# Token mixer with centred small matrices: output held channel by token, channel sums and output projection in fp32, no transposes

## The reference, cut to what matters

```python
x = x + mixer(ln(x)); t = tokens(x); t = t + moe0(ln(t))
x = x + divisive_norm_conv(ln(x)); t = tokens(x); t = t + moe1(ln(t))

def mixer(u):                      # per image, 256 tokens
    xbcdt = u @ W_in               # 128 values, 16 B, 16 C, 8 dt
    dt = softplus(xbcdt[dt] + dt_bias);  dA = dt * (-exp(A_log))
    KV = einsum('bls,blhp->bhsp', B, V * dA)
    y  = einsum('bls,bhsp->blhp', C, KV) + V * D_param
    y  = (y - mean(y)) / sqrt(var(y) + 1e-5) * ln_gamma + ln_beta   # over 128 channels
    return y @ W_out               # 128 -> 64
```

## Time and profile before

| | us |
|---|---|
| median of 3 runs (lowest, highest) | 723.84 (723.64, 726.32) |
| the profiled execution, its own time | 722.71 |
| span of its profile | 720.9 |
| busy: PE, DVE, ACT, POOL | 522.0, 523.4, 378.9, 283.1 |
| mean granted PE clock, of full speed | 0.924 |

### The profile page before, as it was taken

How to read it: one execution, slowest core, us unless ns; L and a number is a source line. 1 busy time by engine, 2 the same in 40 slices (tenths; PEclk the granted TensorE clock), 3 DMA queues, 4 the chain that set the end, 5 groups by cost and what they waited for, 6 DMA issues and landing times.

```text
span 720.9 us, 10179 instructions
## 1 busy us (share of the span) xinstructions
PE 522.0 (72%) x3778; PEld 247.9 (34%) x3778; DVE 523.4 (73%) x926; ACT 378.9 (53%) x440; POOL 283.1 (39%) x240
## 2 busy tenths in 40 slices
PE   2314674578787988798777978797879876975766
PEld 1213232233333433344334333343334332431322
DVE  3266267859798879987988898889979796556413
ACT  2113712467476555756575657664766564643532
POOL 2122146125434463635452653365254433333013
PEclk9999965699998999999999999999999998998788
DMA  4600600063205140505032502450044005500130
GB/s 67 102 3 1 133 0 1 2 132 74 47 1 134 31 89 15 123 13 117 15 83 53 120 16 55 79 119 16 21 99 100 19 17 117 116 18 1 43 76 30
DMA packets 27841, 41.50 MB, mean 58 GB/s; under 512 B 11792, under 2 KB 19088, under 8 KB 27792
## 3 DMA queue, kind: packets, MB, share of 16 engines
q1 hardware_dynamic: 27152, 38.75, 26.2%
q0 software_dynamic: 640, 2.10, 1.0%
HBM read 38.22 MB, written 2.62 MB: 57 GB/s over the span
## 4 chain that ended last, share of the span: by engine, by line
DVE 37%; DMA 23%; PE 13%; issue 10%; POOL 8%; SPq 5%; ACT 4%; POOLq 0%; DVEq 0%; ACTq 0%
DMA WB<-w_scratch 19%; DVE nacc L1134 6%; PE yP L861 4%; PE hP L845 4%; SPq L402 3%; DMA w_scratch<-wTs 3%; DVE YW L1181 2%; POOL stat_c L486 2%; PE sA L760 2%; DVE xsplit L971 2%; PE sA L770 2%; DVE xcen_b L964 2%; POOL stat_b L486 2%; DVE xnrm L964 1%; POOL stat_d L486 1%
## 5 line engine op out<-in xcount | busy, mean ns | idle before, releaser
L691 ACT ACTIVATE H<-hP,b 128x1024 f32<-128x1024 f32 x192 | 209.3, 1111 | 82.4 <-PE hP L845 80.8
L861 PE MATMUL yP<-H,w 128*64 128x512 f32 x768 | 205.6, 618 | 28.5 <-DVE ACC L1181 25.1
L845 PE MATMUL hP<-xT,w 128*64 128x512 f16 x1536 | 212.4, 401 | 4.1 <-ACT H L691 4.0
L556 POOL TENSOR_TENSOR ACC<-ACC,YW 128x512 f32<-128x512 f32 x96 | 125.5, 1313 | 192.1 <-DVE YW L1181 192.1
L845 PEld LDWEIGHTS hP<-xT,w 128*64 128x64 f16 x1536 | 83.6, 114 | 128.0 <-issue 70.8
L1181 DVE SCALAR_TENSOR_TENSOR YW<-yP,b,WB 128x512 f32<-128x512 f32 x96 | 71.3, 744 | 31.9 <-PE yP L861 31.9
L861 PEld LDWEIGHTS yP<-H,w 128*64 128x64 f32 x768 | 54.0, 141 | 71.8 <-issue 38.1
L1134 DVE SCALAR_TENSOR_TENSOR nacc<-PAD,taps,nacc 128x256 f32<-128x256 f32 x112 | 60.5, 540 | 3.7
L1181 DVE SCALAR_TENSOR_TENSOR ACC<-yP,b,WB 128x512 f32<-128x512 f32 x32 | 23.1, 746 | 50.5 <-DMA WB<-w_scratch 50.5
L540 POOL TENSOR_SCALAR nrg<-nacc,go_col 128x512 f32<-128x512 f32 x8 | 12.6, 1573 | 69.1 <-ACT nacc L659 69.1
L578 ACT ACT_TABLE_LOAD x23 | 29.5, 1283 | 9.7 <-DVE nacc L1134 7.9
(11 more groups left out here) (144 smaller groups left out, 775.6 us busy)
## 6 DMA issues: line engine op xcount, KB each, us to landing
WB<-w_scratch SPq DMA_DIRECT2D x32, 1024.0 KB, 10.0
X<-in_x SPq DMA_DIRECT2D x8, 256.0 KB, 12.0
out<-X POOLq DMA_DIRECT2D x8, 256.0 KB, 2.8
H<-in_L_ffn_W SPq DMA_DIRECT2D x2, 512.0 KB, 6.6
H<-in_L_ffn_W SPq DMA_DIRECT2D x2, 256.0 KB, 4.2
w<-in_L_ffn_W SPq DMA_DIRECT2D x1, 512.0 KB, 4.9
w_scratch<-wTs SPq DMA_DIRECT2D x16, 32.0 KB, 1.8
w<-in_L_ffn_W SPq DMA_DIRECT2D x1, 256.0 KB, 4.1
```

What stands on the lines that cost most here:

```text
L556: pool.tensor_tensor(ACC[l][:, cols], ACC[l][:, cols], YW[:, u % 4, :], ALU.add).then_inc(summed, 1)
L691: nc.scalar.activation(H[:, s % RING, :], hP[s % 2][:, :], ACT.Gelu, bias=b1[l][:, e * ch + c:e * ch + c + 1], scale=1.0 / WS)\
L845: mm = nc.tensor.matmul(hP[s % 2][b * C:(b + 1) * C, hf * HALF:(hf + 1) * HALF], w1[l][:, sp, w, b * C:(b + 1) * C], xT[l][g % 2][:, hf * ...
L861: mm = nc.tensor.matmul(yP[hf][a * C:(a + 1) * C, :], w2[l][:, (2 * j + a) * ch + c, :], H[:, (2 * ch * j + 2 * c + a) % RING, hf * HALF:( ...
```

## The change

The output y of the mixer is now made channel by token. V * D becomes a product: the columns of W_in that give V, times D, centred over the 128 channels (`wd`, two fp16 parts), times `xTa`. `KV` is centred over its 128 columns too, so that y comes out of PSUM with mean zero: two fp16 products and one fp32 product of 256 columns for each image. ACT takes y's square and y itself out of PSUM. PE sums the squares over the channels with a column of ones, in fp32 (`y_sums`); DVE scales the sums, POOL takes the power -1/2. `mix_out` multiplies y with `wout_g` in fp32, 8 products instead of 32, and DVE scales the result by the power (first operation) and adds X0b (second). Yd, Yc, ysplit, the transposes `turn_hi` and `turn_lo` and layer norm n's steps on DVE, ACT and POOL are gone. KV's centring is on DVE (`state`: a reduction and one operation) instead of ACT's copy.

The slots: `AB_LEAD` goes from 42 to 36. Modulo 24, on DVE: centre_a 12, sums_a 19, norm_a 22, decay 9, values 10, state 11, y_sums 16, mix_out and what follows it where it was. On PE: proj0, 1, 2 in 5, 7, 8 (before 23, 1, 2), c_cols 9 (3), state 11 (5), y0 12 (6), y1 14 (8), y_sums 16, mix_out 17 (17). On ACT: squares of a 17 (13), proj0, 1, 2 in 5, 6, 7 (23, 0, 1), c_cols and decay 9 (3), y0 12, y1 14. On POOL: low part of a 21 (15), X0b 14 (8), the new power y_sums 16. The start-up is six slots shorter.

```diff
@@ tables
-    ab=dict(turn_a=12, proj0=17, proj1=19, proj2=20, c_cols=21, state=23, y0=24, y1=26, turn_hi=32,
-            turn_lo=34, mix_out=35, turn_b=38, gate=41, send=43),
+    ab=dict(turn_a=13, proj0=17, proj1=19, proj2=20, c_cols=21, state=23, y0=24, y1=26, y_sums=28,
+            mix_out=29, turn_b=32, gate=35, send=36),
...
-    ab=dict(centre_a=0, sums_a=6, norm_a=10, decay=21, values=22, y0=25, y1=27, centre_n=28, sums_n=29,
-            norm_n=30, mix_out=35, centre_b=35, sums_b=36, norm_b=37, top2=41, weights=41),
+    ab=dict(centre_a=0, sums_a=7, norm_a=10, decay=21, values=22, state=23, y_sums=28, mix_out=29,
+            centre_b=29, sums_b=30, norm_b=31, top2=35, weights=35),
...
-AB_LEAD = 42
+AB_LEAD = 36
@@ PE
+                    for t in range(2):
+                        for s in range(2):
+                            nc.tensor.matmul(sA[:, t * PIX:(t + 1) * PIX], wd[:, s, :],
+                                             xTa[:, hf * HALF + t * PIX:hf * HALF + (t + 1) * PIX],
+                                             start=(s == 0), stop=False)
+                        mm = nc.tensor.matmul(sA[:, t * PIX:(t + 1) * PIX], KVs[q, t * INNER:(t + 1) * INNER],
+                                              ctS[q, t * PIX:(t + 1) * PIX], start=False, stop=True)
...
+                elif k == "y_sums":
+                    pe.wait_ge(*a_read(k, g))
+                    pe.wait_ge(yev.sem, yev.at(g))
+                    for t in range(T):
+                        mm = nc.tensor.matmul(sA[:, t:t + 1], ysq[:, t * P:(t + 1) * P], ones[:, 0:1],
+                                              start=True, stop=True)
...
                     for t in range(T):
-                        for n in range(4):
-                            mm = nc.tensor.matmul(sA[:, t * C:(t + 1) * C], yT[:, n // 2, t * P:(t + 1) * P],
-                                                  wout[:, n % 2, :], start=(n == 0), stop=(n == 3))
+                        mm = nc.tensor.matmul(sA[:, t * C:(t + 1) * C], yT[:, t * P:(t + 1) * P], wout_g[:, :],
+                                              start=True, stop=True)
@@ ACT
+                elif k in ("y0", "y1"):
+                    hf = int(k[-1])
+                    cols = slice(hf * HALF, (hf + 1) * HALF)
+                    act.wait_ge(ymm.sem, ymm.at(g, hf + 1))
+                    nc.scalar.activation(ysq[:, cols], sA[:, :], ACT.Square, scale=1.0 / WS).then_inc(yev.sem, 1)
+                    nc.scalar.activation(yT[:, cols], sA[:, :], ACT.Copy, scale=1.0 / WS).then_inc(yev.sem, 1)
@@ POOL
+                elif k == "y_sums":
+                    pool.wait_ge(yvar.sem, yvar.at(g))
+                    pool.tensor_tensor(stat["n"][:, 3, :], stat["n"][:, 2, :], neg_half[:, :], ALU.pow)\
+                        .then_inc(yrs.sem, 1)
@@ DVE
+                elif k == "state":
...
+                    v.tensor_reduce(kv_mean[:, :], state, AX, ALU.add).then_inc(kvC.sem, 1)
+                    dve.wait_ge(kvC.sem, kvC.at(g, 1))
+                    v.scalar_tensor_tensor(out=KVs[:, :].rearrange("p (m n) -> p m n", m=2),
+                                           in0=kv_mean[:, :].unsqueeze(2).to_broadcast([64, 2, INNER]),
+                                           scalar=-1.0 / INNER, in1=state, op0=ALU.mult, op1=ALU.add)\
+                        .then_inc(kvC.sem, 1)
+                elif k == "y_sums":
+                    dve.wait_ge(ysm.sem, ysm.at(g))
+                    v.tensor_scalar(stat["n"][:, 2, :], sA[:, 0:T], 1.0 / INNER, 1e-5, ALU.mult, ALU.add)\
+                        .then_inc(yvar.sem, 1)
...
-                    v.scalar_tensor_tensor(out=X1[g % 2][:, :, :], in0=sA[:, :].rearrange("p (t c) -> p t c", t=T),
-                                           scalar=1.0 / WS, in1=X0b[:, :, :], op0=ALU.mult, op1=ALU.add)\
+                    dve.wait_ge(yrs.sem, yrs.at(g))
+                    v.tensor_tensor(X1[g % 2][:, :, :], sA[:, :].rearrange("p (t c) -> p t c", t=T),
+                                    per_tile(stat["n"][:, 3, :], C), ALU.mult).then_inc(x1s.sem, 1)
+                    dve.wait_ge(x1s.sem, x1s.at(g))
+                    v.tensor_tensor(X1[g % 2][:, :, :], X1[g % 2][:, :, :], X0b[:, :, :], ALU.add)\
                         .then_inc(x1v.sem, 1)
```

More of the change, by code:

```diff
@@ L61 @@
 ACT_AT = dict(
-    ab=dict(sums_a=7, turn_a=12, proj0=17, proj1=18, proj2=19, c_cols=21, decay=21, state=23, sums_n=28,
-            turn_hi=32, turn_lo=33, sums_b=36, turn_b=37, top2=41, send=42),
+    ab=dict(sums_a=5, turn_a=13, proj0=17, proj1=18, proj2=19, c_cols=21, decay=21, y0=24, y1=26,
+            sums_b=30, turn_b=31, top2=35, send=36),
     cd=dict(sums_c=1, turn_c=4, norms=9, sums_d=11, turn_d=14, top2=17, send=18),
@@ L72 @@
 POOL_AT = dict(
-    ab=dict(sums_a=7, norm_a=9, decay=25, state=26, sums_n=30, norm_n=31, sums_b=34),
+    ab=dict(sums_a=7, norm_a=9, state=26, y_sums=28, sums_b=29),
     cd=dict(sums_c=1, norm_c=2, scale=8, sums_d=12),
@@ L76 @@
 SP_AT = dict(
-    ab=dict(decay=22, send=41),
+    ab=dict(decay=22, send=35),
     cd=dict(send=21),
@@ L319, in sums_until @@
             return 6 * (u // 8) + max(0, u % 8 - 1)
-        A_USES = ("turn_a", "proj0", "proj1", "proj2", "c_cols", "state", "y0", "y1", "turn_hi", "turn_lo", "mix_out",
+        A_USES = ("turn_a", "proj0", "proj1", "proj2", "c_cols", "state", "y0", "y1", "y_sums", "mix_out",
                   "turn_b", "gate", "send")
@@ L341, in a_read @@
             count, k = {"turn_a": (trS["a"], 1), "proj0": (pjS, 1), "proj1": (pjS, 2), "proj2": (pjS, 3),
-                        "c_cols": (ctC, 1), "state": (kvS, 1), "y0": (yv, 1), "y1": (yv, 2), "turn_hi": (trS["n"], 1),
-                        "turn_lo": (trS["n"], 2), "mix_out": (x1v, 1), "turn_b": (trS["b"], 1), "gate": (gv[0], 1),
+                        "c_cols": (ctC, 1), "state": (kvC, 2), "y0": (yev, 2), "y1": (yev, 4), "y_sums": (yvar, 1),
+                        "mix_out": (x1s, 1), "turn_b": (trS["b"], 1), "gate": (gv[0], 1),
                         "send": (wts[0], 1)}[name]
@@ L614, in ab @@
                     act.wait_ge(ct.sem, ct.at(g))
-                    nc.scalar.activation(ctS[:, :], sA[0:64, :], ACT.Copy, scale=1.0 / WS).then_inc(ctC.sem, 1)
+                    nc.scalar.activation(ctS[:, :], sA[0:64, :], ACT.Copy).then_inc(ctC.sem, 1)
                 elif k == "decay":
@@ L766, in ab @@
                     pe.wait_ge(*a_read(k, g))
[L767 removed]
+                    pe.wait_ge(kvC.sem, kvC.at(g))
                     q = slice(32 * hf, 32 * hf + STATE)
[L769 to L778 removed]
+                    for t in range(2):
[5 more added lines that the diff above has]
+                                              ctS[q, t * PIX:(t + 1) * PIX], start=False, stop=True)
```

99 lines of the change are left out of this document (31 added, 68 removed).

## The result

The changed kernel takes 740.25 us (median of 4 runs, 737.01 to 742.88), the kernel before 723.74 in the runs beside it (722.27 to 726.32): ratio 1.022, 95% interval 1.016 to 1.028. Slower, as forecast (736, range 712 to 747). The profiled execution took 737.01, its span is 735.2: 14.3 more than before, where the working had 14.0. It is the fastest of the four; by medians the difference is 16.5, and the forecast lay 12.3 above 723.74.

The account below looks back on a forecast made before the run. DVE's nearly gapless work and two DRAM weight transfers bound each frame. Start-up -12.3, frame 0 +1.5, frames 1 to 5 +22.8, frame 6 +2.0 sum to +14.0, 736.7 profiled; forecast 736 us, range 712 to 747.

Parts of the forecast that it names:

- What bounds, and what leaves: Per 24-slot frame (four images), DVE work and two weight transfers set time; the removed normalisation, mostly under a transfer, gains nothing.
- C + D = 28.4, no change: First layer 0 scaling, through layer 1 gate weights (C), to first layer 1 scaling: C's 2.5 gain spent, 28.4 +/- 0.8 us.
- D: Layer 1 weights' DRAM transfer up to first layer 1 scaling, 15.3 us before; PE's new tail, not the DMA, ends it.
- A + 4.55: First layer 1 scaling to layer 0 gate weights (A), 30.7 us before, DVE almost without gap: grows 4.55 a frame.
- B unchanged: Layer 0 weights' DRAM transfer, from gate weights to first layer 0 scaling (B): keeps 15.9 us.
- Start-up -12.3: Up to the first layer 0 scaling: X1 ready 16 earlier, 3.7 given back to norm a steps, so 12.3 us shorter.
- X1 at 42.6: At start-up, X1 ready at 42.6 instead of 58.7 after DVE's operations behind the second X, 16 us earlier.
- Frame 0 +1.5, frame 6 +2.0, end 0: Frame 0, without layer 1, +1.5 us; frame 6, with no group behind it, +2.0; frame 7 and end, without mixer, 0.
- The signs: DVE busy about 6 us less a frame, late transposes releasing layer 1 scaling, weights' copy over 1 late, layer 0 scaling about 78.
- The faster one (702): PE's tail ahead of the first layer 1 scaling doesn't decide, y_sums and pow hide: 702 us, chance 0.22.
- the limit of 15.8: PE's work between layer 1 send and last transposes: below some 15.8 us the faster rival was to hold.
- Rival 3 (clock): PE's 1.2 GHz level lasts through C, D and the head of A: another 2 to 3 us a frame, 749, chance 0.10.

Follow-up runs that it names:

- e8: Changed kernel with the new arithmetic put back in the slots of the kernel before (AB_LEAD 42): 715.8 us, ratio 0.984.
- e10: From e9, state, y0 and y1 also moved late to slots 11, 12 and 14, decay and values staying in 3 and 4: 727.28 us, ratio 1.005.
- e3: Changed kernel with y0 and y1 in slots 14 and 15, y0 behind the late transposes: 748.2 us, ratio 1.032.
- e2: Changed kernel with layer norm a's sums and scaling for the next group moved out of A: 723.79 us, ratio 0.999.
- e9: From e8, y_sums moved late to slot 16 on PE, DVE and POOL, as in the changed kernel: 740.32 us, ratio 1.015.

## Why the prediction was right, point by point

**What bounds, and what leaves.** Right. The removed normalisation was cover: 39 of the 59 us of DVE work left frames 1 to 5, and each of them is longer. e8 shows it from the other side: without that work and in the old slots its best frames are 74.6 and 74.7 and their mean 76.5, against 73.9 to 75.9 and 74.8 before.

**C + D = 28.4, no change.** Right on the path, a little long in size: 28.2 in this frame, 27.5 on average (27.0 to 28.2), where it was 28.7 before, so 1.3 a frame were won. The third unit ran at full clock (389.66, 1.02 us), not at the half clock that one branch of the sum allowed for. D needs both of its new parts to reach 17.3. One is the serial feed, proj, table loads, ctS, decay and Vs, which the six-slot shift moved behind the layer 1 send: without its lateness (e10) D is 15.4. The other is y0 on PE ahead of the transposes: without it (e3) D is 15.9. The prediction had both in one sum and didn't part them.

**A + 4.55.** The mechanism was right, the size too small: +5.6 on average. Up to X1 it is +1.9 (10.1 for 8.2; 1.05 taken). POOL's pow was ready at 9.3, as said (9.2), but PE was later: the y products took 1.9 (1.4 taken; within 1.1 to 2.2) and y_sums 1.95 (1.5 taken; within 0.6 to 2.6). mix_out's 2.0 was as said. Behind X1 it is +3.8 (26.3 for 22.5; 3.5 taken), and here errors of both signs partly cancel. The top-2 up to the weights grew from 5.93 to 6.28, by 0.35 and not 0.7: its slow rows (0.90 and 1.06 for 0.22) are no news, before it had 0.68 and 1.33. The taps were not in the sum: the four behind norm a's new sums take 3.84 (436.36) instead of 2.93, at least 0.9 more in each of frames 2 to 5, and e2, which moves norm a away, has 2.92 again. DVE before, the same taps and the two slow rows:

```profile
429.05 2.93 DVE L1134 SCALAR_TENSOR_TENSOR nacc<-PAD,taps,nacc 128x256 f32<-128x256 f32 x4
...
438.90 0.68 DVE L1004 TENSOR_TENSOR gt<-gt,iota_m 128x64 f32<-128x64 f32 x1
...
440.39 1.33 DVE L1021 TENSOR_TENSOR gt<-gt 128x64 f32<-128x64 f32 x1
```

The steps of e8, e9, e10 and the changed kernel in A (31.5, 33.2, 34.8, 36.4) are not prices of single terms: in that frame of e9 and in e10 X1 waits for POOL's pow behind norm a's low part, in the changed kernel for PE.
y_sums also decides the point at which page and rows were weighed: 0.122 us a record lies near the fp32 transposes (0.165) and far from the fp16 rows (0.035). The Trainium skill, "TensorE: Matmul & The Clock Gate", section on the weight-path modes, has fast weight load off for FP32, and the trace agrees in direction; the prediction's estimate of 1.7 us from the page's time of a weight load is 0.25 short.

**B unchanged.** 15.2 to 16.8, 15.8 on average for 15.4 before: +0.4. By the terms a frame was to grow by 4.55, and it grew by 4.7 (C + D -1.3, A +5.6, B +0.4). That closeness is partly luck: over five frames A's error of 5 us is made up for by C + D's of 6, with B's 2 on top.

**Start-up -12.3.** This step failed in size: -8.3. Two records on PE in the changed kernel:

```profile
37.85 3.54 PE L768 MATMUL sA<-ones,ysq 128*128 128x1 f32 x16 [1.27 <-ACT yT L616]
...
41.65 3.68 PE L774 MATMUL sA<-wout_g,yT 128*128 128x64 f32 x16 [0.26 <-DVE stat_n L1079]
```

The same steps take 1.95 and 2.00 in frames 1 to 6 (3.54 and 3.68 again in frame 0). The step of the working that fails here is "X1 at 42.6": behind the second X it adds up DVE's own operations alone, so PE's y_sums and mix_out stand in it at nothing. DVE waits 2.64 and 1.60 us for them, and X1 is ready at 46.8, 4.2 later. About 3.2 of these are the longer records (7.22 for 3.95 in both); the prediction had named the level of 1.2 GHz as a rival for the frames and not for this place. From X1 ready to the gate weights it takes 19.6 instead of 14.8, +4.8 (3.7 taken), and from there to the first scaling it takes 15.8 instead of 17.0. That makes the 4 us. The mechanism is shown by e10: put `state` back behind centre_a, and the first scaling comes 13 us later than in e8.

**Frame 0 +1.5, frame 6 +2.0, end 0.** Measured -0.3, +3.0, -3.7. The end has the same work in all kernels and took 110.4 here, 114.2 before and 110.7 to 117.4 in the experiments. Before, the last part's second output product took 1.95 us (697.45, with a granted clock of 0.53 from 697 to 700), after it 1.06 (712.93). So the agreement between 14.0 and 14.3 is luck by 3.7 us, which made up for most of the start-up. What made frame 0 1.8 us shorter than forecast stays open.

**The signs.** DVE's busy time fell by 7.8 us a frame (6 said), and late transposes release the first layer 1 scaling, as said. The copy that starts layer 1's transfer came 0.6 us behind its transpose (398.81 to 399.43), not over 1, and the first layer 0 scaling at 82.2, not at 78. The sum gave 736.7 for the profiled execution and so 737.8 for the median; the 736 that was said is not quite that sum.

**The rivals.** The faster one (702) fell at the point that it named: from the layer 1 send to the last transposes PE took 16.3 us (398.54 to 414.82), above the limit of 15.8. e8 comes near that rival by other slots: start-up -12.3 and 1.7 a frame, the upper end of its range. Rival 3 (clock) did not come in the frames of the changed kernel, but in e9's long ones it cost more than was given to it, 4 to 10 us a frame.

## What to carry to other kernels

Work taken off the busiest engine gains only if it stood on the path; ask first what it covered. When an edit changes arithmetic and schedule at once, measure them apart: in the old slots the new arithmetic is 1.6% faster than the kernel before, and the changed slots cost more than that (735.2 against 712.5 us of span). Then ask where such a gain lies: e8's is at start-up and not in the frames. There it hangs on order too, since e10, with `state` behind centre_a, has its first scaling at 91.1, later than the 90.5 before. Whether the old arithmetic would gain the same by another order at start-up was not tried. A step moved later takes its whole serial feed along (copies, table loads), and that feed can be what is late.

## What the runs showed of the hardware that was not expected

**A gap in PE's work can cost more than itself.** In e9 frames 3 and 4 took 75.9 and 77.3 us at a mean granted clock of 0.98 and 0.94, and frames 1, 2 and 5 81.4 to 85.9 at 0.84 to 0.89, with DVE's busy time nearly the same (56.3 to 58.5). PE had idled 2.2 to 3.4 us ahead of A in all five, and the low level came behind each gap (e9 above); why it lasted longer in some is not shown. Whole executions differ too: one of e2's ten took 852.6 us at a mean granted clock of 0.655, the others 721.4 to 729.3 at 0.900 to 0.937. Yet the mean alone is a poor guide: e9's fastest execution (731.32) had the lowest, 0.880. A forecast for a change of under 1% has to be compared frame by frame.

**The granted clock isn't always what the records show.** y_sums and mix_out took 3.54 and 3.68 us at start-up in the changed kernel, in e8 and in e10. In e8 the window 40 to 43 has a granted clock of 0.50, which fits; in the changed kernel the window 37.85 to 45.33 has 1.00, for the same durations. Lengths of known records are the safer reading.

**An fp32 product with one column costs nearly what 64 columns cost**: 1.95 against 2.00 us for 16 records, so here a narrow fp32 sum on PE was priced by the record and not by its columns.
